# Low halves one fill later, seven key jobs beside the selection chain, and tie counts over the whole row

## What is computed

```
x = conv_nonlocal(x)                       # softmax over all pixel pairs, 1x1 convolutions
h = layernorm(tokens(x))
q  = rms(h @ Wcq) @ Wq ; rope              # 16 heads, 32 + 32 dims
k1 = rms(h @ Wckv) @ Wk, rope(h @ Wk_rope) # full causal branch
scores = h @ W_imp
idx = sort(top_k(scores, 256))             # ties go to the earlier token
ks = h[idx] @ Wsel_k ; vs = h[idx] @ Wsel_v
kw = h @ Wwin_k ; vw = h @ Wwin_v          # window branch
out = gated sum of three attentions @ Wproj ; then the experts
```

## Time and profile before

| | |
|---|---|
| Time, median of 3 runs | 2863.33 us (2860.24 to 2863.4) |
| Profiled execution, its own time | 2860.51 us |
| its span | 2858.6 us |
| PE busy | 2337.6 us (82%) |
| DVE busy | 1682.3 us (59%) |
| ACT busy | 1215.4 us (43%) |
| POOL busy | 537.8 us (19%) |
| TensorE clock granted, mean | 0.899 |

### The profile page before, as it was taken

The page is one execution under the profiler, slowest core; times in us unless marked ns, Lnnn a source line. Parts: engine busy times, 40 slices in busy tenths (PEclk is TensorE's granted clock), DMA queues, the critical chain, the costliest instruction groups (busy, mean ns, idle before and its releaser), DMA issues. The chain is left out here.

```text
span 2858.6 us, 46600 instructions
## 1 busy us (share of the span) xinstructions
PE 2337.6 (82%) x16656; PEld 1554.2 (54%) x16656; DVE 1682.3 (59%) x3155; ACT 1215.4 (43%) x2665; POOL 537.8 (19%) x575
## 2 busy tenths in 40 slices
PE   5585867763899999799999799999899999620995
PEld 3354545542566666466566466666566665310884
DVE  4767676764366566366566365665465664550676
ACT  2343333430455555355455355555355555410442
POOL 0133333352011011011011010110010110235332
PEclk8787887885999999899999899999899999755997
DMA  2254545478647546455655465565466461431113
GB/s 94 99 212 164 189 182 196 171 284 204 138 96 145 126 97 138 106 126 109 127 125 119 91 132 125 114 130 117 105 139 125 97 145 37 127 58 52 46 52 108
DMA packets 222862, 360.74 MB, mean 126 GB/s; under 512 B 68794, under 2 KB 124701, under 8 KB 222240
## 3 DMA queue, kind: packets, MB, share of 16 engines
q1 hardware_dynamic: 218304, 349.20, 48.8%
q0 software_dynamic: 4320, 8.43, 0.9%
HBM read 229.58 MB, written 126.56 MB: 125 GB/s over the span
## 5 line engine op out<-in xcount | busy, mean ns | idle before, releaser
L1400 ACT ACTIVATE prob<-ps 128x512 f32<-128x512 f32 (+5 forms) x1600 | 636.5, 441 | 733.5 <-PE ps L1351 587.7
L1453 DVE TENSOR_REDUCE maxima<-ps 128x1 f32<-128x512 f32 (+3 forms) x768 | 387.7, 547 | 293.7 <-PE ps L1279 146.5
L1372 PE MATMUL ps<-prob,plain 128*32 128x512 f32 (+5 forms) x3200 | 512.0, 443 | 0.0
L1423 POOL TENSOR_TENSOR products<-products,sums 128x256 f32<-128x256 f32 x192 | 140.3, 731 | 1604.5 <-DVE sums L1444 1603.2
L1458 DVE TENSOR_REDUCE maxima<-ps 128x2 f32<-128x512 f32 (+1 forms) x512 | 294.2, 608 | 242.9 <-PE ps L1290 99.7
L1444 DVE RECIPROCAL sums<-sums 128x256 f32<-128x256 f32 x192 | 331.5, 1736 | 103.9 <-ACT sums L1411 103.9
L1343 PE MATMUL ps<-q1a_s,k1a_s 128*128 128x512 f32 (+3 forms) x768 | 303.4, 395 | 0.0
L1351 PE MATMUL ps<-q1b_s,k1b_s 128*128 128x512 f32 (+3 forms) x768 | 301.3, 393 | 0.0
L1372 PE MATMUL ps<-prob,v_s 128*32 128x512 f32 (+3 forms) x1536 | 284.4, 491 | 0.0
L1279 PE MATMUL ps<-k1a_s,q1a_s 128*128 128x512 f32 (+3 forms) x768 | 234.4, 375 | 2.8 <-DMA k1a_s<-k1ah_dram 2.8
L1343 PEld LDWEIGHTS ps<-q1a_s,k1a_s 128*128 128x128 f32 x768 | 147.4, 192 | 126.8 <-issue 118.9
(11 more groups left out here) (332 smaller groups left out, 4837.1 us busy)
## 6 DMA issues: line engine op xcount, KB each, us to landing
qh_dram<-pairs SPq DMA_DIRECT2D x96, 512.0 KB, 3.3
kwh_dram<-pairs SPq DMA_DIRECT2D x64, 512.0 KB, 3.0
qa_s<-qh_dram SPq DMA_DIRECT2D x128, 256.0 KB, 4.5
kwa_s<-kwh_dram SPq DMA_DIRECT2D x128, 256.0 KB, 7.4
q1a_s<-qh_dram SPq DMA_DIRECT2D x128, 256.0 KB, 4.7
qb_s<-qh_dram SPq DMA_DIRECT2D x64, 256.0 KB, 9.0
kwb_s<-kwh_dram SPq DMA_DIRECT2D x64, 256.0 KB, 9.9
k1a_s<-k1ah_dram SPq DMA_DIRECT2D x32, 512.0 KB, 6.9
```

What stands on the lines that cost most here:

```text
L1372: mm = pe.matmul(ps[at:at + VD, SCORES + k % 2, q0 - c * CH:q0 - c * CH + w], w_, m.prob[:, n % PROBS, h, 0:w], start=first, stop=True, sk ...
L1400: act.activation(m.prob[:, u % PROBS, h, 0:w], ps[:, turn % SCORES, 0:w], ACT.Exp, scale=SCALE).then_inc(s["exp_done"], 1)
L1423: pool.tensor_tensor(o, o, m.sums[:, br, cc], ALU.mult).then_inc(s["divided"], 1)
L1453: ins = dve.tensor_reduce(partial[:, h, i, part:part + 1], bank[:, 0:w], AX, ALU.max)
```

## The change

Three things change. First, the low half of a `nope` or `abs` fill is a step of its own, `low`, that stands one fill later in the list: DVE no longer stands still for ACT's cast straight after a fill, and one more bank stays undrained in the meantime. The semaphore `emptied_dve` now counts in the order of `LEFT`. Head steps named `low` take the cost 2.0 that the table has for the early step of that name. Second, `KEYS_EARLY` goes from 5 to 7. Third, the counts within a token's own tile (two narrow DVE operations with sums in each of eight `count` steps) are taken out and made up for after `count` 7 by four operations over 128x1024 and one reduction. The cost of `count` is set from 2.6 to 1.8.

```diff
-def head_steps(b, jobs, vals, last):
+def head_steps(b, jobs, vals, last, halves):
     todo = []
     for n, job in enumerate(jobs):
-        todo += fills(b, *job)
+        for x in fills(b, *job):
+            todo.append(x)
+            if halves:
+                todo.append(halves.pop(0))
+            if x[5] in ("nope", "abs"):
+                halves.append(("low",) + x[1:])
         todo.append(("add", b) + job)
...
-        "low": 2.0, "key": 12.0, "count": 2.6, "place": 5.0, "gather": 8.0, "chosen": 1.0}
+        "low": 2.0, "key": 12.0, "count": 1.8, "place": 5.0, "gather": 8.0, "chosen": 1.0}
...
-        two.append(("round", b) + last)
+        two += [("round", b) + last] + halves
...
-KEYS_EARLY = 5
+KEYS_EARLY = 7
...
+LEFT = [x for x in STEPS if x[0] == "low" or x[0] == "fill" and x[5] in ("rope", "rot")]
...
-def by_dve(n):
-    return sum(x[0] == "fill" for x in FILLS[:n])
+def by_dve(fill):
+    return LEFT.index(fill if fill in LEFT else ("low",) + fill[1:]) + 1
...
         if t < NT - 1:
-            dve.tensor_scalar(junk[:, hi:T], e.score[:, hi:T], own, None, ALU.is_gt, ALU.add,
-                              accum_out=e.cnt[:, t, 1:2])
-        dve.scalar_tensor_tensor(out=e.spread[:, t, :], in0=e.score[:, lo:hi], scalar=own, in1=m.below[:],
-                                 op0=ALU.is_equal, op1=ALU.mult, accum_out=e.cnt[:, t, 3:4])
-        run(dve.tensor_scalar(junk[:, lo:hi], e.score[:, lo:hi], own, None, ALU.is_gt, ALU.add,
-                              accum_out=e.cnt[:, t, 2:3]))
+            ins = dve.tensor_scalar(junk[:, hi:T], e.score[:, hi:T], own, None, ALU.is_gt, ALU.add,
+                                    accum_out=e.cnt[:, t, 1:2])
+        run(ins)
+        if t < NT - 1:
+            return
+        tiles = e.score.rearrange("p (t n) -> p t n", t=NT)
+        above = e.junk[1].rearrange("p (t n) -> p t n", t=NT)
+        run(dve.tensor_tensor(e.spread, tiles, each_tile(e.imp, P), ALU.is_equal))
+        run(dve.tensor_tensor(e.spread, e.spread, each_token(m.below[:], NT), ALU.mult))
+        run(dve.tensor_tensor(above, tiles, each_tile(e.imp, P), ALU.is_gt))
+        run(dve.tensor_tensor(e.spread, e.spread, above, ALU.add))
+        run(dve.tensor_reduce(e.cnt[:, :, 2], e.spread, AX, ALU.add))
```

More of the change, by code:

```diff
@@ L331, in phase_steps @@
     for b in range(B):
-        one, last = head_steps(b, keys[:KEYS_EARLY], [("w", t) for t in range(NT)], None)
-        two, last = head_steps(b, keys[KEYS_EARLY:] + rest, [("s", t) for t in range(KEEP // P)], last)
-        two.append(("round", b) + last)
+        halves = []
+        one, last = head_steps(b, keys[:KEYS_EARLY], [("w", t) for t in range(NT)], None, halves)
+        two, last = head_steps(b, keys[KEYS_EARLY:] + rest, [("s", t) for t in range(KEEP // P)], last, halves)
+        two += [("round", b) + last] + halves
         todo += merged(early_steps(b), one)
@@ L749, in early_vector @@
         if t > 0:
-            dve.tensor_scalar(junk[:, 0:lo], e.score[:, 0:lo], own, None, ALU.is_ge, ALU.add,
-                              accum_out=e.cnt[:, t, 0:1])
+            ins = dve.tensor_scalar(junk[:, 0:lo], e.score[:, 0:lo], own, None, ALU.is_ge, ALU.add,
+                                    accum_out=e.cnt[:, t, 0:1])
         if t < NT - 1:
-            dve.tensor_scalar(junk[:, hi:T], e.score[:, hi:T], own, None, ALU.is_gt, ALU.add,
-                              accum_out=e.cnt[:, t, 1:2])
-        dve.scalar_tensor_tensor(out=e.spread[:, t, :], in0=e.score[:, lo:hi], scalar=own, in1=m.below[:],
-                                 op0=ALU.is_equal, op1=ALU.mult, accum_out=e.cnt[:, t, 3:4])
-        run(dve.tensor_scalar(junk[:, lo:hi], e.score[:, lo:hi], own, None, ALU.is_gt, ALU.add,
-                              accum_out=e.cnt[:, t, 2:3]))
+            ins = dve.tensor_scalar(junk[:, hi:T], e.score[:, hi:T], own, None, ALU.is_gt, ALU.add,
[10 more added lines that the diff above has]
+        run(dve.tensor_reduce(e.cnt[:, :, 2], e.spread, AX, ALU.add))
     elif name == "place":
@@ L817, in _ @@
                     sp.dma_start(kept[b].gates, m.gates[:]).then_inc(s["k1_kept"], 16)
-                elif step in HALVES_OF:
-                    n = HALVES_OF.index(step)
+                elif step[0] in ("low", "round"):
                     if step[0] == "round":
+                        n = HALVES_OF.index(step)
                         _, _, kind, g, c = step
@@ L824, in _ @@
                     else:
+                        n = HALVES_OF.index(("fill",) + step[1:])
                         _, _, kind, g, c, comp = step
                         k = 2 if comp == "nope" and kind == "q" else 0
-                        sp.wait_ge(s["emptied_dve"], by_dve(FILLS.index(step) + 1))
+                        sp.wait_ge(s["emptied_dve"], by_dve(step))
                     dst = {"q": kept[b].q, "k": kept[b].kw, "s": kept[b].ks}[kind]
@@ L914, in _ @@
                         act.copy(hi, ps[:, 4 + f % BANKS, 0:width(step[2])]).then_inc(s["hi_done"], 1)
-                elif step[0] not in ("fill", "add"):
+                elif step[0] not in ("fill", "low", "add"):
                     nonlocal_scalar(act, m, s, step)
@@ L928, in _ @@
                     w = width(kind)
-                    pool.wait_ge(s["emptied_dve"], by_dve(FILLS.index(("fill", b, kind, g, c, "rot")) + 1))
+                    pool.wait_ge(s["emptied_dve"], by_dve(("fill", b, kind, g, c, "rot")))
                     if j >= 2:
@@ L947, in _ @@
                     early_vector(dve, m, s, run, *step[1:])
[L948 removed]
+                elif step in LEFT:
                     _, b, kind, g, c, comp = step
[L950 removed]
+                    n = FILLS.index(("fill",) + step[1:])
                     w = width(kind)
                     bank = ps[:, 4 + n % BANKS, 0:w]
[L953 removed]
                     if comp in ("rope", "rot"):
+                        dve.wait_ge(s["fill_ready"], n + 1)
                         j = ADDS.index(("add", b, kind, g, c))
@@ L960, in _ @@
                     else:
-                        k = HALVES_OF.index(step)
+                        k = HALVES_OF.index(("fill",) + step[1:])
                         hi, lo = pair(k, kind)
```

2 lines of the change are left out of this document (1 added, 1 removed).

## The result

The changed kernel takes 2893.28 us, median of 4 runs (2887.72 to 2893.4); the kernel before has 2861.78 beside it (4 runs, 2857.88 to 2863.4). The ratio is 1.0107, interval [1.009, 1.0125]: 1% slower. The profiled span goes from 2858.6 to 2891.1. The forecast was 2875, with 2888 as its upper end: right in sign, half in size.

What follows compares the result with a forecast made beforehand. In the heads stage the chain bounds the E half, PE the N half's score units, stores the last batch. +4.15 us a batch, three times 12.5, plus 2.5 makes +15 on 2860.51: 2875.5; range 2854 to 2888.

Steps and rivals of the forecast that it cites:

- Key: E half up to the key's end: POOL's add of k01 slows a key operation; +1.0 us, bounds 0 and 1.3.
- Key to the first count: E half: five head operations instead of four, in an order that waits for casts and banks; +3.0 us, bounds 0.6 and 4.
- Counts and ties: E half: eight narrow pairs out, five wide passes in, one held by POOL's subtraction; +2.4 us.
- Place to gather: E half, up to the gather: no cast wait and no POOL add during place; -1.4 us, bounds 0 and -3.
- the N half: From the gather to the next squares: 2.1 + 0.3 + 0.5 - 1.65 - 2.1 = -0.85 us a batch.
- the two waits: N half: PE waits of 2.1 us at the k31 rot fill and 2.3 at the fifth q fill.
- gather to proj: Gather to the next proj: two more fills on PE and a bank wait; +2.1 us, bounds 1.4 and 2.5.
- rival 3: N half: new PE stalls drop the granted clock, +4 us in each of three batches, 2887; chance 0.12.
- The last batch: Last batch alone, paced by stores: -2.5 us after the gather, +2.5 with the gather 5.0 later.
- the clock of the E half rises: E half: more jobs fill PE's gaps and raise its clock; up to -25 us, 2851; chance 0.2.
- A draw by a missed collision: POOL's operations miss the wide passes and key, casts come early; 2856, or 2866 with half of it; chance 0.2.

Runs made afterwards that it cites:

- e6: The changed kernel with POOL's wide subtraction for the gather's low half issued after its work for count 1 instead of with place; 2882.24 us, ratio 1.0088.
- s3: The changed kernel with k30's low half moved ahead of proj and that of q20's abs ahead of the first y on DVE; 2867.27 us, ratio 1.0022.
- e5: The changed kernel with the narrow tie pairs back in place of the wide passes; 2881.68 us, ratio 1.0081.
- s1: The changed kernel with narrow tie pairs, and the low halves of k30 and q20's abs moved ahead of proj and the first y; 2860.45 us, ratio 0.9997.
- s4: The changed kernel with narrow tie pairs, the two low halves moved, and POOL's wide subtraction moved to its work for count 1; 2857.38 us, ratio 0.9985.
- e1: The kernel before with KEYS_EARLY 7 alone, low halves inside their fills and narrow ties; 2861.91 us, ratio 1.001.
- g3: The changed kernel with narrow tie pairs and low halves right behind their own fill in both halves, weights kept; 2861.61 us, ratio 1.0002.
- g1: The changed kernel with narrow tie pairs, low halves late in the E half only; 2867.62 us, ratio 1.0026.
- g2: The changed kernel with narrow tie pairs, low halves late in the N half only; 2865.28 us, ratio 1.0021.
- e3: The kernel before with late low halves alone, five jobs, narrow ties, old count cost, remaining early low halves ahead of the last vals; 2855.9 us, ratio 0.9987.
- e8: The changed kernel with the new low steps weighing nothing in the merge of the step lists; 2898.28 us, ratio 1.014.

## Why the forecast was right in sign and short in size

Batch 1, in the steps of the prediction. In the E half:

- **Key.** The add beside the key did cost 1.0 (L724, 1.37 for 0.42). But the key began a whole us earlier, at 12.68 after `squares` and not 13.66, so the net is -0.06 for +1.0.
- **Key to the first count.** +3.28 for +3.0; DVE waits 5.34 us before the first fill and 1.81 before the k11 rope drain.
- **Counts and ties.** +2.19 for +2.4. One pass at 3.25, the others at 1.22 to 1.24; e6 shows the cause. (The sums that went out were not mostly of one input, as the prediction says: of each pair one, L755, has two, and it is the one that the earlier trace rows show held.)
- **Place to gather.** -0.44 for -1.4. The add (L947) does hold a small operation: L785 takes 0.96, 0.32 more than in the kernel before. But POOL's next operation, the remainder L954 from 307.24 to 308.58, holds the first four L788 as well: 2.15 where the next four take 1.13. I had not priced that.

The gather is thus 4.97 later for 5.0, from terms off by up to 1.1 that cancel: the mechanisms were right in the main, the closeness of the sum is luck.

The step that failed is **the N half, and in it the price of the two waits**. The forecast for this half was 2.1 + 0.3 + 0.5 - 1.65 - 2.1 = -0.85 a batch. Measured are 2.58 + 0.51 + 0.19 - 1.18 = +2.10 in batch 1, +1.96 in batch 0 and +1.89 in batch 2. That makes 8.5 of the 17.5 us by which the sum fell short of the span.

I forecast waits of 2.1 and 2.3 at the k31 rot fill and the fifth q fill; they are 2.06 and 2.40, at those fills. What I set against them was their own length. With the waits gone and all else the same (s3), batch 1 is 6.76 us shorter from proj to the next `squares`: 2.33 to the first score, 3.22 to the second y, 1.21 after it. That is 1.5 times the 4.46 of idle time. All batches say the same: from proj to the next `squares`, the nine with both waits (after, e5, e6) take 89.2 to 91.4 us, mean 89.9, and the twelve without (s1 to s4) 81.9 to 83.9, mean 82.6. That is 7.2 a batch for 4.46.

The stretch from gather to proj is no part of that price, though s3 has it 0.66 shorter than the changed kernel in batch 1. It took +2.58 for my +2.1, but it has two lengths, 7.8 to 8.0 and 8.5 to 8.6, with the waits and without them: the changed kernel's batch 0 has 7.78, s1's three have 8.62, 7.85 and 8.62.

Of the 2.3 us that batch 1's waits cost beyond their own length, 1.7 are PE's own busy time for the same instructions (22.08 + 31.80 + 14.99 = 68.87 in s3, 21.48 + 32.62 + 16.47 = 70.57 in the changed kernel), most of it at a lower clock in the last stretch, as in rival 3. That rival had it with 0.12 and +4 a batch. The low clock isn't spread as that rival had it: in the stretch up to the first score it is 0.91 with the wait and 0.88 without, and e5, which has the same waits, spends 34.07 us of PE on 100 instructions that cost 32.62 in the changed kernel, and 14.71 instead of 16.47 in the last stretch. Batch 2 of s1, with neither wait, has a last stretch of 15.82 busy at 0.73. Where the clock falls varies from kernel to kernel and from batch to batch, so 7.2 is the mean of these runs and no constant.

Taken without waits, my terms for this half were good: s3 has -1.82 from proj to the first score for -1.8 (= 0.3 - 2.1), -3.03 from there to the second y for -3.45 (= -1.8 - 1.65), and -2.25 from there to the statistics (11.55 to 9.30) for -2.1. In the changed kernel that last term was -1.17.

**Batch 0** lost 9.2, not 4.15. Besides the N half, its gather comes 7.3 later than before and not 5.0: at 61.62, 2.2 later than batch 1's. In s3, with the same E half, it comes at 59.83. So most of the 2.2 is probably a variation of the run, not an effect of the change; with one profile of each that is not shown.

**The last batch** lost 5.7 for +2.5: its gather is 5.0 later than before and then 0.7 more is lost, where I had -2.5. This is the second step that failed: I set the late low halves at nothing here. The runs price them. From the last gather to the end of the heads stage, before takes 61.9 us. Seven jobs with no low half late take 58.5 (e1) and 58.8 (g3), so one job less in the stores is worth 3.1 to 3.4, somewhat more than I had. With one half late it is 60.1 (g1, g2), and with both late 62.1 to 63.1 in all eight kernels that have it (62.6 in the changed kernel, 63.1 in s3). Five jobs go from 61.9 to 63.9 with late low halves (e3). ACT's casts are first held by a store of the steady rhythm at 648.90, 24 us after the gather,

```profile
648.90 0.58 ACT L929 CAST pairs<-ps 128x512 fp32r<-128x512 f32 x1 [1.98 <-DMA qh_dram<-pairs]
...
652.76 0.58 ACT L929 CAST pairs<-ps 128x512 fp32r<-128x512 f32 x1 [1.96 <-DMA qh_dram<-pairs]
```

and from there 3.86 us pass per three pairs, 1.29 each, as in the earlier trace rows. In e1 and g3 a store holds them from 20 us after the gather. So the rate was right and the stores get going 4 us too late. In the changed kernel PE waits 1.38, 0.92 and 0.82 us for low halves (L979) ahead of 648.90, and e1 and g3 have no such wait there; that these waits are the whole of the 4 us is argued, not shown.

**The unchanged rest** took 3.7 more. Over all 16 profiled executions after that of before it varies from 2196.9 to 2204.9, and not with the loss (e8, as slow as the changed kernel, has 2198.9), so some us of any single span are no effect. That (3.7), the E half of batch 0 (2.3) and the last batch (3.2) make the other half of what the sum missed.

The rivals: that the clock of the E half rises (0.2) is wrong: the first eight of the gather's matmuls take 2.08 us as before, and the E half's mean clock is 0.70, where it was 0.73. A draw by a missed collision (0.2) is wrong: POOL's L938 hit and cost 2.0 for the 2.2 forecast. Only the third, that stalls cost clock, had a part.

## What to carry to other kernels

Look for where a deferred drain lands: one operation that frees a bank, queued behind other work on its engine (4.5 us of it at y), and one more behind proj, cost three batches 22 us (269.8 us from proj to the next `squares` in the changed kernel, 247.5 with the two moved), while the same deferral elsewhere cost little (and some 4 us in the last batch). The place changes with every number in the plan. A stall on the engine that bounds a stretch is to be priced above its own length; here 4.5 us of it came back as 7. Read more than one batch before a stretch is called shorter. And parts that are draws one by one say little about them together.

## What the runs showed of the hardware

- DVE and POOL delay each other, and the later one waits for nearly all of the other's operation: POOL's 2.34 us operation took 3.32 behind a running DVE pass, and the next DVE pass 3.25 instead of 1.23 behind it.
- `TENSOR_SCALAR` on 128x256 from SBUF, with one large input, was held as well (four took 2.15 us beside POOL's L954, 1.13 after it), and so was a `TENSOR_TENSOR` on 128x8 beside POOL's add (0.96, its neighbour 0.17). Operations that read PSUM kept their times beside the same POOL operations (L974 at 275.83, 0.68 beside an L954 of 275.53), and so did the summing counts (L758 on 128x896 at 291.03, 1.15 beside an L954 of 291.11).
- A pass of two inputs over 128x1024 in f32 takes 1.22 to 1.24 us, and a reduction of it 1.22 (L768 to L772 where nothing holds them).
